# A graph network in four layers: the second layer's weight net moved into the first layer's second gather

## The chip, the cores and the metric

The program runs on one core of one Trainium2 chip (trn2). The metric is device time in microseconds, the median of the runs shown. The engines of the core are TensorE (PE, with its weight loads apart as PEld), VectorE (DVE), ScalarE (ACT), GpSimd (POOL) and SyncE (SP), and 16 DMA engines serve them.

## The reference

Four graph layers on 3125 nodes with 256 features and 100,000 edges; after each, a layer norm of x plus the layer's output. Two of them matter here.

```
# layer 0 (graph convolution)
norm = edge_weight * rsqrt(deg_out[src] * deg_in[dst] + EPS)
h6 = relu(segment_sum((x @ W6)[src] * norm, dst) + b6)
h7 = relu(segment_sum((h6 @ W7)[src] * norm, dst) + b7)
out = h7 @ Wp + bp
# layer 1, the weights of each edge
h = silu(edge_attr_8 @ fc_w1 / sqrt(8))        # 8 -> 64
h = silu(h @ fc_w2 / 8)                        # 64 -> 64
w = h @ fc_w3 / 8                              # 64 -> 256, one row per edge
```

The three lines of layer 1 are the "weight net" of this document. They depend on the edge's eight attributes and on nothing else; layer 1's later stage multiplies w with gathered rows.

## The kernel before, in words

The program is written by hand, engine by engine: each helper writes the instructions of one engine, in the order in which they run there, with semaphores between them. A meeting of all engines (`meet`) divides it into stages. Around the change they are:

1. **Preparation** (to some 2470 us). Edges are counted and ranked; POOL scatters a record of 16 numbers per edge, sorted by source (`rec_s`), then one of 8 numbers, sorted by destination (`rec_d`), to DRAM, by indirect DMAs of 128 records each (L334).
2. **The weight net** (`mlp_vector`, `mlp_sync`, `mlp_tensor`, `mlp_scalar`; L716 to L837). 832 chunks of 128 edges, in 104 groups of eight. For a group SP loads 64 KB of records (L747); PE transposes them (L771, bank 0), makes the first product in four matmuls of 128 columns (L779, bank 1), the second in one of 512 columns (L788, bank 4) and, chunk by chunk, the third, 64 rows by 256 columns (L797, banks 5 to 7). Even chunks take rows 0 to 63 of the array, odd ones rows 64 to 127. A float32 matmul stands in the profile as two passes, each with a weight load. ACT copies the transposed records (L811), applies silu (L818, L826), and writes a chunk's weights out of the bank, scaled and unscaled (L835, L837). SP stores a group, 1 MB, to `weights_dram` (L752). The steps are pipelined by numbers: in step n PE does the transposing for chunk n-5, the first product for n-7, the second for n-10 and the third for n-14. When the net is done, PE transposes the degrees (L801), DVE copies them (L728) and SP spreads them through DRAM to all partitions (L755, L757).
3. **Layer 0, first gather**: x rows are gathered (L1029), multiplied by a one-hot matrix (L1121) and added (L1086).
4. **The product with W6** (`linear_tensor`, L906 and L914; `linear_keep`, L922; `relu_bias_vector`, L935 and L937), and the store of the table h6 to DRAM (`write_table`, L890).
5. **Layer 0, second gather** (`gather_pool`, `second_vector`, `second_tensor`). POOL gathers 128 rows of h6 per chunk, 808 chunks, into a ring of 22 slots (L1160). DVE makes the weighted one-hot matrix of a chunk (L1171); PE multiplies it with the gathered rows (L1194), two chunks to a bank, eight banks; after each pair `pe.drain()` raises the semaphore `summed` (L1196). On it wait POOL, for a free slot, and DVE, which adds a chunk's sums to the block's rows (L1182), 16 chunks behind its one-hot matrices. At its start SP loads all records `rec_s` (6.6 MB) for layer 1 (L1207) and that layer's weights.
6. **Products with W7 and Wp, layer norm**, then layer 1, which waits for the records in `y_vector` (L1294), and gathers its own rows (L1363) beside the weights of each edge.

The lines of the second gather that the steps speak of:

```
pe.matmul(half_bank(c), hot20[:, c % 20, :], hg[:, c % R2, :], start=True, stop=True)
if c % 2 == 1:
    pe.drain().then_inc(summed.s, 1)
```

Of the kernel before, what the change touches and what calls it, by code (L numbers as in the profile page):

```python
# [13 lines left out]
P = 128  # L14
N, E, D = 3125, 100000, 256
NB = -(-N // P)
# [7 lines left out]
MUL = 64  # L24
# [62 lines left out]
def program(nc, t, out):  # L87
    with ExitStack() as ctx:
# [602 lines left out]
        o = 0  # L691
# [8 lines left out]
        RW = 16  # L700
        w_out = cut(acc, o, RW * D, RW, D)
        o += RW * D
# [4 lines left out]
        assert o <= DIN  # L707
        fc_all = acc[:, o - 512 - P - D:o]
        din_t, din_row = ring[0:NB, 5200:5200 + P], acc[:, DIN:DIN + NPAD]
# [10 lines left out]
        def mlp_vector():  # L720
            v.wait_ge(scattered_s.s, 16 * EJ)
            v.memset(fc_all, 0.0).then_inc(fc_zeroed.s, 1)
            v.wait_ge(fc_in.s, 16 * 18)
            then_v(v.tensor_scalar(fc3, fc3, 0.125, None, ALU.mult))
            v.tensor_scalar(fc3[:, 2 * MUL:3 * MUL], fc3[:, 2 * MUL:3 * MUL], 0.5773502691896258, None,
                            ALU.mult).then_inc(fc_scaled.s, 1)
# [3 lines left out]
        def mlp_sync():  # L730
            sp.wait_ge(scattered_s.s, 16 * EJ)
            sp.wait_ge(fc_zeroed.s, 1)
# [3 lines left out]
            for k in range(2):  # L736
                sp.dma_start(fc2[k * MUL:(k + 1) * MUL, k * MUL:(k + 1) * MUL],
                             t["L1_gnn_fc_w2"]).then_inc(fc_in.s, 16)
                for to, part in enumerate((2, 0, 3, 1)):
                    sp.dma_start(fc3[k * MUL:(k + 1) * MUL, to * MUL:(to + 1) * MUL],  # L740
                                 t["L1_gnn_fc_w3"][:, part * MUL:(part + 1) * MUL]).then_inc(fc_in.s, 16)
            for n in range(NG + 2):
# [7 lines left out]
                if i >= 0:  # L750
# [3 lines left out]
            sp.wait_ge(din_ready.s, 1)  # L754
            sp.dma_start(din_dram, din_t).then_inc(din_out.s, 16)  # L755
            sp.wait_ge(din_out.s, 16)
            sp.dma_start(din_row, din_dram.rearrange("(o b) p -> o (b p)", o=1).to_broadcast([P, NPAD])  # L757
                         ).then_inc(din_in.s, 16)

        def mlp_tensor():  # L760
            pe.wait_ge(deg_kept.s, 1)
            pe.wait_ge(fc_scaled.s, 1)
            for n in range(8 * NG + 14):
                i = n // 8
                c = n - 5
                if c >= 0 and c % 8 == 0 and c // 8 < NG:
                    i = c // 8
                    pe.wait_ge(rec_b_in.s(i, 3), rec_b_in.n(i, 3))
# [3 lines left out]
                c = n - 7  # L772
                if c >= 0 and c % 8 == 0 and c // 8 < NG:
                    i = c // 8
                    pe.wait_ge(rec_kept.s, i + 1)
                    if i >= 1:
                        pe.wait_ge(first_act.s, i)
                    for j in range(4):
                        ins = pe.matmul(ps[1][:, j * P:(j + 1) * P], fc1[:, j, :], rec_t[:, i % 2, :],  # L779
                                        start=True, stop=True)  # L780
                    ins.then_inc(first_done.s, 1)
                c = n - 10
                if c >= 0 and c % 8 == 0 and c // 8 < NG:
                    i = c // 8
                    pe.wait_ge(first_act.s, i + 1)
                    if i >= 1:
                        pe.wait_ge(second_act.s, i)
# [1393 lines left out]
```

## Time and profile before

| what | value |
|---|---|
| median of 3 runs | 10671.05 us (10670.89 to 10685.13) |
| the profiled execution, its own time | 10728.81 us |
| its span | 10726.9 us |
| mean granted clock of TensorE | 0.766 |
| PE busy | 6037.8 us, 56% |
| DVE busy | 5900.6 us, 55% |
| POOL busy | 5661.9 us, 53% |
| ACT busy | 2871.8 us, 27% |

The busy shares are means over stages with different limits; no engine is busy throughout. A row of the profile names the line, the engine, what is written and read, and the count; behind the bar stand busy time, the mean of one instruction and the engine's idle time before them with what ended it. "issue" is idle time for which the profile shows no cause. PEq is PE's sequencer, where a drain stands. A clock of 1.00 is TensorE at 2.4 GHz, 0.50 is 1.2 GHz, and a value between is a mix of the two.

### The profile page before, as it was taken

The numbers are of one execution on the slowest core, as the hardware profiler recorded it, in microseconds if no ns is written. First come the engines' busy times: TensorE is split into PE (matmuls) and PEld (weight loads), VectorE is DVE, ScalarE is ACT, GpSimd is POOL, SyncE is SP. The second block draws the span as 40 slices with busy tenths as digits, with TensorE's granted clock in tenths as the row PEclk, the third lists the DMA queues.
The fourth block names the chain that finished last, engine by engine and source line by source line (L and its number), as shares of the span: only waits on it lengthen the run. The fifth ranks groups of instructions, "written<-read, shape, count | busy, mean of one in ns | idle before, by whom it ended". The sixth has DMA issues, their size and how long they took to land. (4 is left out here: it accounts for less than half of the span.)

```text
span 10726.9 us, 101982 instructions
## 1 busy us (share of the span) xinstructions
PE 6037.8 (56%) x21277; PEld 3348.6 (31%) x21277; DVE 5900.6 (55%) x17189; ACT 2871.8 (27%) x9329; POOL 5661.9 (53%) x5879
## 2 busy tenths in 40 slices
PE   2211344446865555555556777774555578845564
PEld 1101233334433333333333111153333334333332
DVE  8925533430016666544446999946656579942223
ACT  0000000106852222100004888842222236600000
POOL 5776656561006666566652777723555520046664
PEclk9999855558986666666677999976666669966666
DMA  2000111104553333433334777734666646523333
GB/s 78 6 6 5 32 46 46 46 31 132 175 192 93 93 94 93 111 91 92 91 78 109 213 213 213 214 79 129 186 187 187 187 127 175 158 77 92 92 92 81
DMA packets 796197, 1192.44 MB, mean 111 GB/s; under 512 B 161213, under 2 KB 631923, under 8 KB 788941
## 3 DMA queue, kind: packets, MB, share of 16 engines
q0 software_dynamic: 259712, 606.96, 21.8%
q1 hardware_dynamic: 535885, 578.95, 16.7%
q8 instruction: 197, 3.23, 0.1%
q14 instruction: 403, 3.30, 0.1%
HBM read 926.73 MB, written 258.64 MB: 111 GB/s over the span
## 5 line engine op out<-in xcount | busy, mean ns | idle before, releaser
L1160 POOL DMA_INDIRECT ring<-scaled_table,idx_s x832 | 789.4, 949 | 1170.0 <-DVEq L193 771.5
L1029 POOL DMA_INDIRECT big<-x_table,rec_d_sb x808 | 808.9, 1001 | 1086.3 <-DMA x_table<-big 721.3
L1758 POOL DMA_INDIRECT ring<-att_table,rec_d_sb x808 | 776.5, 961 | 810.8 <-DVE acc L1868 277.6
L1437 PE MATMUL bank<-ring,wts 128*128 128x512 f32 x1664 | 929.6, 641 | 401.2 <-DVE acc L1424 174.3
L1363 POOL DMA_INDIRECT ring<-y_table,idx_s x832 | 805.0, 968 | 462.8 <-DVEq L193 184.0
L334 POOL DMA_INDIRECT rec_s<-acc,big x784 | 844.4, 1077 | 373.6 <-issue 253.3
L334 POOL DMA_INDIRECT rec_d<-x_res,big x784 | 753.1, 961 | 496.9 <-issue 249.1
L1160 POOL DMA_INDIRECT ring<-h_table,rec_d_sb x808 | 766.6, 949 | 454.5 <-issue 223.7
L2111 PE MATMUL bank<-ring,acc 128*128 128x256 f32 x1664 | 692.1, 558 | 522.5 <-issue 505.6
L1121 PE MATMUL bank<-big,acc 128*128 128x256 f32 x1616 | 644.5, 539 | 573.7 <-issue 450.8
L1194 PE MATMUL bank<-ring,acc 128*128 128x256 f32 x1616 | 642.1, 537 | 542.9 <-issue 477.4
L1382 ACT ACTIVATE ring<-ring,big 128x64 f32<-128x64 f32 x2496 | 686.6, 339 | 257.5 <-issue 148.6
L1777 PE MATMUL bank<-big 128*128 x2424 | 624.3, 388 | 206.6 <-issue 124.0
L1182 DVE TENSOR_TENSOR acc<-acc,bank 128x256 f32 x808 | 340.5, 421 | 615.7 <-PEq L1196 334.8
L2111 PEld LDWEIGHTS bank<-ring,acc 128*128 128x128 f32 x1664 | 407.5, 271 | 807.1 <-issue 748.7
L2101 DVE TENSOR_TENSOR acc<-acc,bank 128x256 f32 x416 | 175.2, 421 | 859.5 <-PEq L2114 656.4
L1121 PEld LDWEIGHTS bank<-big,acc 128*128 128x128 f32 x1616 | 381.6, 261 | 836.4 <-issue 787.3
L1194 PEld LDWEIGHTS bank<-ring,acc 128*128 128x128 f32 x1616 | 380.4, 261 | 804.6 <-issue 748.2
L401 ACT COPY big<-bank 128x425 f32<-128x425 f32 x49 | 25.2, 515 | 2215.2 <-PE bank L456 1659.4
L1437 PEld LDWEIGHTS bank<-ring,wts 128*128 128x128 f32 x1664 | 249.7, 189 | 1080.5 <-issue 521.1
L1996 PE MATMUL bank<-ring 128*128 128x264 f32 x1616 | 546.1, 426 | 65.5 <-issue 58.8
L1865 DVE TENSOR_TENSOR ring<-bank,wts 128x256 f32<-128x256 f32 x808 | 337.9, 418 | 441.1 <-ACT wts L1819 228.9
(346 smaller groups left out, 12793.6 us busy)
## 6 DMA issues: line engine op xcount, KB each, us to landing
weights_dram<-acc SPq DMA_DIRECT2D x104, 1024.0 KB, 4.5
ring<-weights_dram SPq DMA_DIRECT2D x832, 128.0 KB
rows_spill<-ring SPq DMA_DIRECT2D x808, 128.0 KB
big<-rows_spill SPq DMA_DIRECT2D x808, 128.0 KB, 2.2
ring<-key_dram SPq DMA_DIRECT2D x49, 1024.0 KB
big<-dl_dram SPq DMA_DIRECT2D x50, 512.0 KB
ring<-y_table,idx_s POOLq DMA_INDIRECT x832
ring<-scaled_table,idx_s POOLq DMA_INDIRECT x832
```

What stands on the lines that cost most here:

```text
L334: g.indirect_dma_start(out=table, out_offset=bass.IndirectOffsetOnAxis(ap=row_of[k][:, j:j + 1], axis=0), in_=stage[:, j, :], in_offset=No ...
L1029: g.indirect_dma_start(out=xg[:, c % RG, :], out_offset=None, in_=x_table, in_offset=bass.IndirectOffsetOnAxis(ap=recd3i[:, c, D_IDX:D_IDX ...
L1121: pe.matmul(half_bank(c), onehot[:, c % 16, :], xg[:, c % RG, 0:D], start=True, stop=True)
L1160: g.indirect_dma_start(out=slot[:, c % ring_len, :], out_offset=None, in_=table, in_offset=bass.IndirectOffsetOnAxis(ap=index(c), axis=0)) ...
L1194: pe.matmul(half_bank(c), hot20[:, c % 20, :], hg[:, c % R2, :], start=True, stop=True)
L1363: g.indirect_dma_start(out=yg[:, n % RY, :], out_offset=None, in_=y_table, in_offset=bass.IndirectOffsetOnAxis(ap=idx_s[:, n:n + 1], axis= ...
L1382: ins = a.mul(dots[:, c % 2, d * MUL:(d + 1) * MUL], vectors[:, d * MUL:(d + 1) * MUL], recs3[:, c, S_SH + 1 + d:S_SH + 2 + d])
L1437: pe.matmul(ps[6 + u % 2], oh1[c // 4 % 2][:, c % 4, :], mid[:, c % 2, 0:512], start=(c % GS == 0), stop=(c % GS == GS - 1)).then_inc(summ ...
L1758: g.indirect_dma_start(out=ag[:, n % R3, :], out_offset=None, in_=att_table, in_offset=bass.IndirectOffsetOnAxis(ap=recd3i[:, n, D_IDX:D_I ...
L1777: ins = pe.matmul(ps[c % 3][:, 0:TW], hot_n[:, i % 3, k * P:(k + 1) * P], big_b[:, bass.ds(at + s * TW, TW)], start=(s == 0), stop=(s == 2))
L1996: pe.matmul(ps[c % 8][:, 0:TW], oh3[c // 4 % OH3][:, c % 4, :], msg[:, c % 8, :], start=True, stop=True).then_inc(summed.s, 1)
L2111: pe.matmul(ps[u % 8][:, 0:D], oh20[:, c % 20, :], sg[:, c % R4, :], start=(c % 2 == 0), stop=(c % 2 == 1))
```

## The change

The net has no stage of its own any more. Its weights are loaded and scaled in the stage of the product with W6 (`mlp_weights_sync`, `mlp_weights_vector`), and its steps are woven into the second gather: before each chunk's matmul PE does one of the 846 steps, at 38 of the 808 chunks two. ACT's part runs through that stage, and SP's loads and stores too, with the load of all records behind the last store. The net has four banks left, one for transposing, first and second product together and three for the third, and the gather's sums have four instead of eight; DVE adds them eight chunks behind its one-hot matrices instead of 16. A pair's last matmul raises `summed` itself, without a drain. The degrees' transposing, copy and DMAs stand at the end of preparation. The net's output ring `w_out` lies in `big`, and the table h6 behind it.

```diff
-        def mlp_vector():
-            v.wait_ge(scattered_s.s, 16 * EJ)
-            v.memset(fc_all, 0.0).then_inc(fc_zeroed.s, 1)
+        def din_vector():
             v.wait_ge(din_turned.s, 1)
             v.tensor_copy(din_t, ps[4][0:NB, 0:P]).then_inc(din_ready.s, 1)
...
+        turned_bank, first_bank, second_bank = ps[4][:, 0:P], ps[4], ps[4]
+        third_bank = [ps[5 + c][:, 0:D] for c in range(3)]
...
-            for n in range(8 * NG + 14):
+        MLP_STEPS = 8 * NG + 14
+
+        def mlp_tensor_step(n):
...
-                    if i >= 1:
-                        pe.wait_ge(rec_kept.s, i)
-                    pe.transpose(ps[0][:, 0:P], rec_b[:, i % 3, :], ident).then_inc(rec_turned.s, 1)
+                if i >= 1:
+                    pe.wait_ge(second_act.s, i)
+                pe.transpose(turned_bank, rec_b[:, i % 3, :], ident).then_inc(rec_turned.s, 1)
...
-        mlp_vector()
-        mlp_sync()
-        mlp_tensor()
-        mlp_scalar()
-        v.wait_ge(w_stored.s(NG - 2, 2), w_stored.n(NG - 2, 2))
-        v.wait_ge(w_stored.s(NG - 1, 2), w_stored.n(NG - 1, 2))
+        din_vector()
+        din_sync()
+        din_tensor()
+        v.wait_ge(scattered_s.s, 16 * EJ)
...
         linear_scalar()
+        v.memset(fc_all, 0.0).then_inc(fc_zeroed.s, 1)
+        mlp_weights_sync()
         h6_vector()
         linear_over()
+        mlp_weights_vector()
         write_table(h6_table, h6)
...
-            for n in range(NCD + 16):
+            for n in range(NCD + 8):
...
-                c = n - 16
+                c = n - 8
...
-                    ins = v.tensor_tensor(here, here, half_bank(c), ALU.add)
+                    ins = v.tensor_tensor(here, here, quarter_bank(c), ALU.add)
...
         def second_tensor():
+            pe.wait_ge(fc_scaled.s, 1)
+            step = 0
             for c in range(NCD):
+                while step * NCD < (c + 1) * MLP_STEPS:
+                    mlp_tensor_step(step)
+                    step += 1
                 p = c // 2
                 pe.wait_ge(gathered.s(c, R2), gathered.n(c, R2))
                 if c % 2 == 0:
                     pe.wait_ge(weighed.s, weighed.n(p + 1))
-                    if p >= 8:
-                        pe.wait_ge(added.s, added.n(p - 7))
-                pe.matmul(half_bank(c), hot20[:, c % 20, :], hg[:, c % R2, :], start=True, stop=True)
+                    if p >= 4:
+                        pe.wait_ge(added.s, added.n(p - 3))
+                ins = pe.matmul(quarter_bank(c), hot20[:, c % 20, :], hg[:, c % R2, :], start=True, stop=True)
                 if c % 2 == 1:
-                    pe.drain().then_inc(summed.s, 1)
+                    ins.then_inc(summed.s, 1)
...
         def second_sync():
-            sp.wait_ge(table_out.s, table_out.n(0))
-            sp.dma_start(big[:, 0:NCS * RS], by_rank(rec_s_dram)).then_inc(rec_in.s, 16)
...
+            mlp_sync()
+            sp.wait_ge(table_out.s, table_out.n(0))
+            sp.wait_ge(w_stored.s(NG - 2, 2), w_stored.n(NG - 2, 2))
+            sp.wait_ge(w_stored.s(NG - 1, 2), w_stored.n(NG - 1, 2))
+            sp.dma_start(big[:, 0:NCS * RS], by_rank(rec_s_dram)).then_inc(rec_in.s, 16)
...
         second_tensor()
+        mlp_scalar()
```

PE's order in the net's stage before, one group of eight (each row a matmul of the program, x3 the same three times, with the semaphores that it waits for):

```order
L771 MATMUL bank<-ident,acc 128x128 [waits rec_kept,rec_b_in2]
L797 MATMUL bank<-acc 128x256 [waits w_kept]
L797 MATMUL bank<-acc 128x256 [waits w_kept,second_act]
L779 MATMUL bank<-acc 128x128 [waits first_act,rec_kept]
L779 MATMUL bank<-acc 128x128 x3
L797 MATMUL bank<-acc 128x256 [waits w_kept] x3
L788 MATMUL bank<-acc 128x512 [waits second_act,first_act]
L797 MATMUL bank<-acc 128x256 [waits w_kept] x3
```

And in the second gather now, where L1205 is the gather's matmul, L801 the net's third product, L785 the first and L792 the second:

```order
L1205 MATMUL bank<-ring,acc 128x256 [waits added,weighed,gathered10]
L785 MATMUL bank<-acc 128x128 [waits rec_kept]
L785 MATMUL bank<-acc 128x128 x3
L801 MATMUL bank<-acc 128x256 [waits w_kept]
L1205 MATMUL bank<-ring,acc 128x256 [waits gathered11]
L801 MATMUL bank<-acc 128x256 [waits w_kept]
L1205 MATMUL bank<-ring,acc 128x256 [waits added,weighed,gathered12]
L801 MATMUL bank<-acc 128x256 [waits w_kept]
L1205 MATMUL bank<-ring,acc 128x256 [waits gathered13]
L792 MATMUL bank<-acc 128x512 [waits first_act]
L801 MATMUL bank<-acc 128x256 [waits w_kept]
L1205 MATMUL bank<-ring,acc 128x256 [waits added,weighed,gathered14]
```

Third products that stood side by side now have a gather matmul between them. SP's queue from the product with W6 on, in the change: the net's weights (L740 to L746) stand ahead of the store of the table (L889), and loads and stores of groups behind the weights of layer 1.

```order
L740 DMA acc<-in_L_gnn_fc_w 8x64 [waits fc_zeroed,engines_met]
L740 DMA acc<-in_L_gnn_fc_w 8x64 x7
L743 DMA acc<-in_L_gnn_fc_w 64x64
L746 DMA acc<-in_L_gnn_fc_w 64x64 x4
L743 DMA acc<-in_L_gnn_fc_w 64x64
L746 DMA acc<-in_L_gnn_fc_w 64x64 x4
L889 DMA h_table<-big 128x25x256 [waits table_ready]
```

Before, nothing stood between the meeting and that store on this queue, and the load of all records came right behind it.

## Rows read from the trace of the kernel before

**Rows 1.** Stretches: length; busy PE, PEld, DVE, ACT, POOL; clock; DMA share; GB/s.
```profile
2471.00:3144.00 673.00, 557.62 (x2793) 326.97 (x2791) 0.28 (x1) 533.91 (x1972) 0.34 (x1) 0.97 0.52 173
4431.00:5606.00 1175.00, 642.09 (x1616) 380.39 (x1616) 559.31 (x1601) 0.00 (x0) 766.65 (x808) 0.68 0.34 97
5800.00:7000.00 1200.00, 867.74 (x1558) 232.30 (x1556) 1103.19 (x3308) 974.72 (x3306) 852.63 (x973) 1.00 0.73 213
```
**Rows 2.** Timeline of POOL (start, duration, in us), the last scatter.
```profile
2470.38 0.96 POOL L334 DMA_INDIRECT rec_d<-x_res,big  x1 [0.30 <-issue]
```
**Rows 3.** Timeline of DVE, the first instruction after the net's stage.
```profile
3144.52 5.39 DVE L1035 MEMSET x_res<- 128x6400 f32 x1 [6.07 <-issue]
```
**Rows 4.** Waits, second gather, 4431 to 5612 us (total, times, longest).
```profile
PE bank L1194 <- issue: 477.4, 366, 7.4
```
**Rows 5.** Timeline of POOL inside the second gather.
```profile
5001.79 0.95 POOL L1160 DMA_INDIRECT ring<-h_table,rec_d_sb  x1 [0.30 <-issue]
...
5006.08 0.95 POOL L1160 DMA_INDIRECT ring<-h_table,rec_d_sb  x1 [2.10 <-PEq L1196]
```
**Rows 6.** Timeline of PE at the same place (x4 is one pair).
```profile
5006.02 2.04 PE L1194 MATMUL bank<-ring,acc 128*128 128x256 f32 x4 [6.00 <-issue]
5008.29 2.04 PE L1194 MATMUL bank<-ring,acc 128*128 128x256 f32 x4 [0.23 <-issue]
```
**Rows 7.** By line: shortest/median/longest in ns, first and last start in us.
```profile
L1160 POOL DMA_INDIRECT ring<-h_table,rec_d_sb x808: 943/949/1009, 4431.8 to 5586.8; - x162
...
L1182 DVE TENSOR_TENSOR acc<-acc,bank x808: 420/422/423, 4451.0 to 5605.9; 128x256 f32 x162
...
L1196 PEldq DRAIN  x404: 952/2047/8945, 4448.4 to 5603.2; - x135
```
**Rows 8.** DMA issues: KB each, median us to landing.
```profile
weights_dram<-acc SPq DMA_DIRECT2D x104, 1024.0 KB, 4.5
...
big<-rows_spill SPq DMA_DIRECT2D x808, 128.0 KB, 2.2
```
**Rows 9.** Timeline of SP: four of the net's weight loads; the table's store.
```profile
2454.84 4.97 SPq L740 DMA_DIRECT2D acc<-in_L_gnn_fc_w  x4
...
4420.16 0.36 SPq L890 DMA_DIRECT2D h_table<-big  x1
```
**Rows 10.** The gather's start: stretch as in rows 1; PE's second chunk.
```profile
4431.00:4459.00 28.00, 9.73 (x19) 5.54 (x20) 5.60 (x17) 0.00 (x0) 20.83 (x22) 0.50 0.93 348
...
4448.45 1.22 PE L1194 MATMUL bank<-ring,acc 128*128 128x256 f32 x2 [5.03 <-DMA ring<-h_table,rec_d_sb]
```
**Rows 11.** Timeline of PE in the product with W6, at full clock.
```profile
4395.93 1.03 PE L914 MATMUL bank<-wts,ring 128*128 128x256 f32 x4
4396.80 0.38 PE L906 MATMUL bank<-ident,acc 128*128 128x128 f32 x2
```
**Rows 12.** Timeline of PE in the net's stage, one group.
```profile
2800.61 0.33 PE L771 MATMUL bank<-ident,acc 128*128 128x128 f32 x1 [1.06 <-DMA acc<-rec_s]
2800.86 0.70 PE L797 MATMUL bank<-acc 64*128 64x256 f32 x4
2801.50 1.16 PE L779 MATMUL bank<-acc 128*128 128x128 f32 x8
2802.58 1.13 PE L797 MATMUL bank<-acc 64*128 64x256 f32 x6
2803.64 1.13 PE L788 MATMUL bank<-acc 128*128 128x512 f32 x2
2804.70 1.13 PE L797 MATMUL bank<-acc 64*128 64x256 f32 x6
```
**Rows 13.** PE's unexplained waits in layer 1's gather and layer 2's sums.
```profile
PE bank L1437 <- issue: 74.9, 90, 1.6
...
PE bank L1996 <- issue: 58.8, 60, 1.5
```
**Rows 14.** Timeline of DVE, the first use of the loaded records.
```profile
5684.03 0.88 DVE L1295 COPY idx_s<-big 128x832 int32<-128x832 int32 x1 [0.19 <-POOLq L193]
```

More of the change, by code:

```diff
@@ L753, in mlp_sync @@
                                  w_out[:, 8 * (i % 2):8 * (i % 2) + 8, :]).then_inc(w_stored.s(i, 2), 16)
[L754 to L762, printed above, removed]
-            for n in range(8 * NG + 14):
[L764 to L768, printed above, removed]
-                    if i >= 1:
-                        pe.wait_ge(rec_kept.s, i)
-                    pe.transpose(ps[0][:, 0:P], rec_b[:, i % 3, :], ident).then_inc(rec_turned.s, 1)
[L772 to L787, printed above, removed]
-                    pe.matmul(ps[4], fc2, h1[:, i % 2, :], start=True, stop=True).then_inc(second_done.s, 1)
-                c = n - 14
-                if 0 <= c < NCS:
-                    i, k = c // 8, c % 8
-                    half = slice((k % 2) * MUL, (k % 2) * MUL + MUL)
-                    if k == 0:
-                        pe.wait_ge(second_act.s, i + 1)
-                    if c >= 3:
-                        pe.wait_ge(w_kept.s, c - 2)
-                    pe.matmul(ps[5 + c % 3][:, 0:D], h2[half, i % 2, (k // 2) * P:(k // 2) * P + P],
-                              fc3[half, :], start=True, stop=True).then_inc(third_done.s, 1)
-            pe.wait_ge(deg_kept.s, 1)
-            pe.wait_ge(second_act.s, NG)
-            pe.transpose(ps[4][0:NB, 0:P], deg_d[:, 0:NB], ident).then_inc(din_turned.s, 1)
@@ new lines, in program @@
+        MLP_STEPS = 8 * NG + 14
+        def mlp_tensor_step(n):
+            c = n - 5
+            if c >= 0 and c % 8 == 0 and c // 8 < NG:
+                i = c // 8
+                pe.wait_ge(rec_b_in.s(i, 3), rec_b_in.n(i, 3))
+                if i >= 1:
+                    pe.wait_ge(second_act.s, i)
+                pe.transpose(turned_bank, rec_b[:, i % 3, :], ident).then_inc(rec_turned.s, 1)
+            c = n - 7
+            if c >= 0 and c % 8 == 0 and c // 8 < NG:
+                i = c // 8
+                pe.wait_ge(rec_kept.s, i + 1)
+                for j in range(4):
+                    ins = pe.matmul(first_bank[:, j * P:(j + 1) * P], fc1[:, j, :], rec_t[:, i % 2, :],
+                                    start=True, stop=True)
+                ins.then_inc(first_done.s, 1)
+            c = n - 10
+            if c >= 0 and c % 8 == 0 and c // 8 < NG:
+                i = c // 8
+                pe.wait_ge(first_act.s, i + 1)
+                pe.matmul(second_bank, fc2, h1[:, i % 2, :], start=True, stop=True).then_inc(second_done.s, 1)
+            c = n - 14
+            if 0 <= c < NCS:
+                i, k = c // 8, c % 8
+                half = slice((k % 2) * MUL, (k % 2) * MUL + MUL)
+                if k == 0:
+                    pe.wait_ge(second_act.s, i + 1)
+                if c >= 3:
+                    pe.wait_ge(w_kept.s, c - 2)
+                pe.matmul(third_bank[c % 3], h2[half, i % 2, (k // 2) * P:(k // 2) * P + P],
+                          fc3[half, :], start=True, stop=True).then_inc(third_done.s, 1)
@@ L803, in mlp_scalar @@
         def mlp_scalar():
-            for n in range(8 * NG + 14):
+            for n in range(MLP_STEPS):
                 c = n - 5
@@ L810, in mlp_scalar @@
                         a.wait_ge(first_done.s, i - 1)
-                    a.copy(rec_t[:, i % 2, :], ps[0][:, 0:P]).then_inc(rec_kept.s, 1)
+                    a.copy(rec_t[:, i % 2, :], turned_bank).then_inc(rec_kept.s, 1)
                 c = n - 7
```

42 lines of the change are left out of this document (27 added, 15 removed).

## The prediction

> **What bounds the kernel now.** I read the table of stretches first, since one core runs a row of stages divided by meetings of all engines, and a stage is worth what its own last wait is worth [rows 1]. Three stretches matter. The weight net of the second layer (2471 to 3144 us) is a stage in which POOL is idle (one instruction), DVE is idle, and PE and ACT work alone at a granted clock of 0.97. The second gather of the first layer (4431 to 5606) has the opposite mix: ACT idle, POOL 767 us, PE 642 us at a clock of 0.68, DVE 559 us. The third is the second layer's own gather (5800 to 7000), a witness: it moves 213 GB/s with a DMA share of 0.73, and POOL still issues 778 gathers in 1200 us.
>
> Then I read where the net's stage begins and ends. POOL's last scatter of destination records starts at 2470.38 [rows 2]; and DVE opens the next stage with a memset at 3144.52, after 6.07 us of idling in which the last stores land [rows 3]. Only the last few scatters overlap the net.
>
> Last, the gather: PE's unexplained waits of 477.4 us in 366 places [rows 4], then a piece of the timeline. POOL needs 0.95 us for a gather and 0.30 to the next while nothing holds it, and then waits 2.10 us for PE's sequencer, which frees ring slots [rows 5]. At that moment PE has started nothing for 6.00 us [rows 6]: the wait ends for both when a drain ends. The 404 drains reach 8.9 us, with a median of 2.05 [rows 7]. So POOL could do the 808 gathers in 808 x 1.2525 = 1012 us; from first to last they take 1155 (4431.8 to 5586.8) [rows 7], because PE stops now and then at a drain.
>
> **The change, part by part.** The sum is made on the profiled execution, 10728.8 us, which is 57.8 above the median of the three runs.
>
> *The net's stage goes: 670 us saved.* DVE now enters the meeting when the last destination scatter has landed. Its issue starts at 2470.38; a landing takes between 2.2 us (rows read back from the spill) and 4.5 us (a store of 1 MB) [rows 8]. I take the small end, since a scatter moves 4 KB, and 1 us for the meeting: the memset starts near 2474 instead of 3144.5, so 670, with 668 and 671 as ends. The transposing of the degrees, DVE's copy and the two DMAs go ahead of it, on PE, DVE and SP, which wait there for nothing but the scatters. The broadcast of 1.6 MB thereby leaves the window in which x and the records are loaded. It is worth between 0 and 5 us (1.6 MB at the 348 GB/s of [rows 10]); I take 3.
>
> *The weights of the net are loaded under the first product: 1 us lost.* DVE's memset of 896 columns stands ahead of its first addition, which waits for PE's first product anyway. The 18 DMAs stand on SP ahead of the store of the table: four took 4.97 us to issue, so 18 take 22 [rows 9]. They start near 4390 and end near 4412; SP's next work, the table's store, was issued at 4420.16 [rows 9]. Cover is 8 us; were SP twice as slow, the table would be 14 us late. DVE's two short scalings come after its last block and only delay its entry to the meeting, while the table is still on its way. Ends 0 and 14; I take 1.
>
> *The gather takes the net's work.* Its terms, engine by engine.
> POOL: unchanged, 1012 us if never held.
> PE, at full clock: a pass of 256 columns takes 0.217 us (four from 4395.93 to 4396.80, and between full-height products of different kinds nothing is lost) [rows 11]. A chunk of the gather is two passes, 0.434, x 808 = 351 us. A third-layer product of the net is two such passes too. In the old stage it costs less: three of them take 1.06 us (2802.58 to 2803.64) [rows 12], since two neighbours use different halves of the rows and run at once: 0.43 for the two, 0.43 for the third, and 0.2 left, which I read as two changes between half-height and full-height at 0.1 each. In the new order a gather chunk, of full height, stands between any two of them, except at some 38 places where two steps fall together (846 steps on 808 chunks). So 832 x 0.434 = 361 us, plus two changes per chunk, 808 x 0.2 = 162. Per group of eight, the first product takes 1.08, the second 1.06 and the transpose 0.25 [rows 12]; less one change each, counted already, 2.09 x 104 = 217. Less 38 x 0.5 for the neighbours that still pair: PE needs 351 + 361 + 162 + 217 - 19 = 1072 us.
> The Trainium skill (TensorE: Matmul & The Clock Gate, "Part 3: Packing small matmuls") says that matmuls in different row groups run at once in the array. By it this interleaving gives away a gain which the old stage had, and the trace agrees: three products in 1.06 us, where two gather chunks take 0.87.
> ACT: 534 us in the old stage [rows 1]; it has 1080 now, and what waits for it stands three or four steps, 4 to 5 us, behind its cause. Hidden.
> DVE: 559 us for 808 chunks [rows 1], 1.4 per pair. PE may now be only three pairs ahead of it instead of seven; that is still 8 us. Hidden; if DVE fell behind, PE and with it POOL would wait for the banks.
> SP and the DMAs: a store of 1 MB, landing in 4.5 us [rows 8], and a load of 64 KB per eight steps, now every 10.4 us instead of 6.5. In the old stage PE waited 1.06 us for such a load [rows 12], with a group every 6.5 us (673/104); with one every 10.4 the same eight steps of lead leave 3 us to spare. SP's own waits for `w_kept` hold nothing else on its queue but loads and stores of the net and, last, the records' load. The share of DMA becomes 0.34 x 1175/1080 + 0.52 x 673/1080 = 0.69, under the witness's 0.73.
> The drain goes: a matmul tells of its own end, as in the witness and in the sums of the third layer, and there PE's unexplained waits are never longer than 1.6 and 1.5 us [rows 13], against 7.4 here [rows 4]. I count no stall of that kind. The clock: PE has work for 1072 of 1080 us, which is more than in the net's stage with 0.97 and the witness with 1.00 [rows 1], so full clock.
> The largest is PE with 1072. The load of 6.6 MB of records no longer stands beside the first gathers (the second chunk was used only at 4448.45) [rows 10]; PE begins near 4434.5, a landing after POOL, and DVE ends 2 us behind PE. End: 4434.5 + 1072 + 2 = 5508 instead of 5606.3: 98 saved. Ends: 156 saved when POOL bounds (1012 + 7 us), 288 lost when the old stalls return whole (second rival).
>
> *The records' load* is issued when the last store has landed, some 6 us after the gather. The one beside the first gathers was over within the 28 us of [rows 10], and DVE uses it 78 us after the gather's end, at 5684.03 [rows 14]. Hidden; without that cover, 34 us.
>
> Sum: 10728.8 - 670 - 3 + 1 - 98 = 9959, less 57.8: **9901 us**.
>
> **Rivals.**
> *POOL is the bound.* If the changes of height cost nothing, PE needs 910 us and POOL sets the end at 1012 + 7: 9901 - 58 = 9843. For it: the pure pace of [rows 11]. Against: the 0.2 us in [rows 12].
> *The stalls belong to the gather, not to the drain.* Then 477 - 404 x 0.23 (the ordinary drain [rows 6]) = 384 us are added to a PE that is now the bound: 9901 + 384 = 10285; half of them give 10093. For: all three stages with stalls gather through POOL. Against: so does the witness, without any.
> *Stores and gathers add.* While 6.6 MB were loaded beside the first gathers, the DMA share was 0.93 and PE waited 5.03 us for the second chunk [rows 10]. Were every store to hold the gathers for its 4.5 us, POOL's 1012 would grow by 468, to 1480: 10300. The ring of 22 chunks (27 us) speaks against it. The Trainium skill (DMA: Bandwidth & Descriptors, "Queues, rings and completion order") has each DMA engine take whole packets from one queue before it turns to the next; by that rule a store gets more than half of an engine, which is this case in a milder form, and the start of the gather agrees with it.
> *The clock stays at its low level: slower.* If PE runs the woven stream at 1.2 GHz, as it does for much of the gather now (clock 0.68), passes double: 2 x (351 + 361 + 217 - 19) + 162 = 1982 us, a stage of 1989, 814 longer than now: 10671 - 672 + 814 = 10813. It decides from a stage of 1847 us on, that is with the low level over more than 85% of it. For: short waits on ACT, SP and POOL are spread through the stream. Against: the net's stage has the same waits and 0.97.
> *The stage is not freed.* Something under the net other than its own work would have to end late; [rows 2] show nothing.
>
> **How the numbers follow.** PE-bound as computed, 0.55 (9870 to 9960); POOL-bound, 0.20; stalls return in part or whole, 0.14; stores and gathers add, 0.05; low clock, 0.04; not freed, 0.02. A measurement of this kernel tells 0.2%, 21 us, from no change. Faster 0.95, same 0.01, slower 0.04. The range runs from 9830 (POOL-bound, with the small terms at their good ends) to 10080, which takes in stalls up to nearly half and leaves out some 0.18.
>
> **What would show it.** DVE's memset of x near 2474; no net rows before 3000 us. In the gather: duration near 1078, clock above 0.95, POOL's waits on PE's matmuls some 60 us in all, PE's idle small with no wait over 3 us, the third product's passes 0.22 apart and 0.3 before a gather chunk. Wrong: a gather over 1250 us, a clock under 0.85, PE waits of 4 us and more, or POOL never waiting.

## Result, and the profile after

The changed kernel takes 10135.2 us (median of four runs, 10106.9 to 10168.3) against 10671.6 for the one before: a ratio of 0.949, 95% interval 0.947 to 0.952. 536 us are saved where 770 were foretold. The profiled execution took 10106.9 us, its span is 10105.0. The net's old stage is gone as foretold; the second gather, which was to become 98 us shorter, became 110 longer.

The two traces side by side, by first and last starts on their timelines (us, from the span's start):

| stretch | before | after | change | foretold |
|---|---|---|---|---|
| start to POOL's last scatter | 2470.4 | 2459.5 | -10.9 | 0 |
| from there to the first gather of x | 722.2 | 55.4 | -666.8 | -673 |
| first gather stage, to the product with W6 | 1197.0 | 1195.2 | -1.8 | 0 |
| product, table, to the second gather's first | 42.2 | 42.8 | +0.6 | +1 |
| second gather, to DVE's last addition | 1174.5 | 1284.2 | +109.7 | -98 |
| layer 2, to the products after its gather | 1486.1 | 1492.0 | +5.9 | 0 |
| those products, to the next stage's first gather | 246.4 | 185.4 | -61.0 | 0 |
| the rest | 3388.1 | 3390.5 | +2.4 | 0 |

The row of -61 is no work of the change. Its products, 600 passes after layer 2's gather, are the same in both kernels; the table of stretches (columns as in [rows 1]) shows their clock, before and after:

```profile
7088.00:7230.00 142.00, 135.01 (x600) 125.05 (x600) 23.76 (x56) 44.89 (x152) 0.00 (x0) 0.51 0.00 1
```
```profile
6524.00:6604.00 80.00, 73.98 (x600) 70.28 (x600) 23.52 (x54) 43.78 (x147) 0.00 (x0) 0.98 0.00 1
```

600 passes at clock 0.51 take 135 us, at 0.98 they take 74. The level differs from one execution to the next, with no tie to the change: in the trace of `before_again` (below), the same kernel as before, the passes take 75 us at clock 0.97, and the row from them to the next gather is 185 us, as after the change. So the execution profiled before had most likely a slow draw of this stage; it lay 57 us above its median; the one after lies 28 below its own, for a reason that its trace alone does not show. So 621.9 (span to span) - 57 - 28 = 537, the 536 of the medians.

The stretches of the second gather after the change:

```profile
3753.00:3853.00 100.00, 68.26 (x150) 35.18 (x150) 22.07 (x64) 17.50 (x53) 51.08 (x54) 0.57 0.32 95
3853.00:4996.00 1143.00, 1138.68 (x4159) 601.38 (x4159) 522.21 (x1504) 542.64 (x1870) 712.12 (x753) 1.00 0.60 182
4996.00:5037.00 41.00, 38.02 (x117) 19.62 (x117) 13.84 (x39) 15.62 (x55) 2.12 (x3) 0.88 0.47 102
```

For 1143 us (the middle row) PE is busy nearly all the time (1138.68) at full clock, as foretold, and yet gets only 753 chunks done: 1.518 us each, not the 1072/808 = 1.327 of the prediction. The first 100 us carry 32 chunks (51 us lost against the steady pace), the last 41 carry 23 (6 lost). 808 x 1.518 + 51 + 6 = 1284.

The stage by line (busy, mean in ns | idle before, releasers), and PE's waits (total, times, longest) in it:

```profile
L1162 POOL DMA_INDIRECT ring<-h_table,rec_d_sb x808 | 765.4, 947 | 550.0 <-PE bank L1205 275.8 <-issue 202.7 <-DMA h_table<-big 66.8
L1205 PE MATMUL bank<-ring,acc 128*128 128x256 f32 x1616 | 576.7, 440 | 18.5 <-DMA ring<-h_table,rec_d_sb 16.9 <-issue 1.6
L801 PE MATMUL bank<-acc 64*128 64x256 f32 x1664 | 575.4, 436 | 0.0
```
```profile
PE bank L1205 <- DMA ring<-h_table,rec_d_sb: 16.9, 2, 16.5
PE bank L779 <- issue: 14.5, 1, 14.5
PE bank L785 <- ACT acc L812: 8.6, 1, 8.6
PE bank L792 <- ACT acc L819: 5.1, 4, 2.7
```

The 477 us of unexplained waits of [rows 4] have shrunk to some 17, all but one of them short; POOL now waits 276 us for PE's sums, where some 60 were foretold. The stage is bound by PE. PE's timeline shows where its time goes (start, duration):

```profile
4205.93 0.70 PE L801 MATMUL bank<-acc 64*128 64x256 f32 x2
4206.56 0.70 PE L1205 MATMUL bank<-ring,acc 128*128 128x256 f32 x2
4207.09 1.05 PE L785 MATMUL bank<-acc 128*128 128x128 f32 x8
4208.08 0.70 PE L801 MATMUL bank<-acc 64*128 64x256 f32 x2
4208.70 0.70 PE L1205 MATMUL bank<-ring,acc 128*128 128x256 f32 x2
4209.33 0.70 PE L801 MATMUL bank<-acc 64*128 64x256 f32 x2
```

From a half-height product (64 rows, L801) to a full-height one (L1205) and back it is 0.63 us each time. Two passes of 256 columns are 0.434 [rows 11], so a change of height costs some 0.19, not the 0.1 of the prediction.

### The profile page after: what moved, and what is told of

The parts are those of the page before. It is cut to its first block and busy times, and to the rows that moved or that the text cites. A ratio compares the mean times of both kernels' runs of the same rounds, so it can differ in the third digit from the quotient of the medians.

```text
span 10105.0 us, 101372 instructions
## 1 busy us (share of the span) xinstructions
PE 6039.2 (60%) x21277; PEld 3249.0 (32%) x21277; DVE 5884.0 (58%) x17189; ACT 2904.1 (29%) x9330; POOL 5654.3 (56%) x5879
## 5 line engine op out<-in xcount | busy, mean ns | idle before, releaser
L2126 PE MATMUL bank<-ring,acc 128*128 128x256 f32 x1664 | 695.6, 560 | 519.8 <-issue 500.6
L2126 PEld LDWEIGHTS bank<-ring,acc 128*128 128x128 f32 x1664 | 409.0, 272 | 806.4 <-issue 744.9
L1834 ACT ACTIVATE wts<-bank 128x256 f32<-128x256 f32 x808 | 302.7, 383 | 1001.7 <-remote 460.3
L1205 PE MATMUL bank<-ring,acc 128*128 128x256 f32 x1616 | 576.7, 440 | 18.5 <-DMA ring<-h_table,rec_d_sb 16.9
```

Source lines behind the costliest of these rows:

```text
L1205: ins = pe.matmul(quarter_bank(c), hot20[:, c % 20, :], hg[:, c % R2, :], start=True, stop=True)
L2126: pe.matmul(ps[u % 8][:, 0:D], oh20[:, c % 20, :], sg[:, c % R4, :], start=(c % 2 == 0), stop=(c % 2 == 1))
```

## Experiments

The result and the experiments fall into six sets of runs. In each set the kernel before was timed on the same chip as the others, and its times are of two kinds: 10671, 10624, 10629 and 10675 us in four sets (the first is that of the result above), 8989 and 8991 in two. The five sets of the experiments ran on five different chips, none of them twice, so whether those are two sorts of chip or one in two conditions, the runs cannot tell. I call them the *late* and the *prompt* condition, for a reason that the traces give below. Ratios are against the kernel before of the same set. A length given for the gather runs from POOL's first gather to DVE's last addition. Where no ratio is given below, a kernel ran only once (full_nogather, before_nogather, before_again, filler_again, nogather_again, filler_2, nogather_2).

### Full height, pairs, and the drain

**full_height**: zeros fill the other half of the weights, so every product has 128 rows.

```diff
-        fc2, fc3 = acc[:, o:o + P], acc[:, o + P:o + P + D]
+        fc2, fc3 = acc[:, o:o + P], acc[:, o + P:o + P + 2 * D]
...
-                pe.matmul(third_bank[c % 3], h2[half, i % 2, (k // 2) * P:(k // 2) * P + P],
-                          fc3[half, :], start=True, stop=True).then_inc(third_done.s, 1)
+                pe.matmul(third_bank[c % 3], h2[:, i % 2, (k // 2) * P:(k // 2) * P + P],
+                          fc3[:, (k % 2) * D:(k % 2) * D + D], start=True, stop=True).then_inc(third_done.s, 1)
```

> The changed kernel, but each third-layer product runs over all 128 rows against weights whose other half is zero, so that PE never changes between half-height and full-height products; their number, order, waits and banks stay. Theory H (each change of height costs 0.19 us on PE, two per chunk): PE needs 0.87 + 2.1/8 = 1.13 us per chunk, POOL with its 1.2525 sets the pace, the second gather shrinks from 1284 us to 1012 plus some 45 for its start, about 1060, and the kernel takes 9880 to 9940. Rival S (the 0.19 us belongs to any switch between two kinds of product, with its bank and its semaphore wait): nothing changes, 1284 us and 10107 to 10168.

Measured (late condition): 10019.3 us, ratio 0.9436 (0.9414 to 0.9458); gather 1226 us. PE and ACT on the timeline:

```profile
4209.88 0.59 PE L801 MATMUL bank<-acc 128*128 128x256 f32 x2
4210.31 0.59 PE L1205 MATMUL bank<-ring,acc 128*128 128x256 f32 x2
...
4210.74 1.05 PE L786 MATMUL bank<-acc 128*128 128x128 f32 x8
...
4211.63 0.60 PE L801 MATMUL bank<-acc 128*128 128x256 f32 x2
4212.06 0.59 PE L1205 MATMUL bank<-ring,acc 128*128 128x256 f32 x2
...
4213.79 0.59 PE L1205 MATMUL bank<-ring,acc 128*128 128x256 f32 x2
4215.65 0.60 ACT L819 ACTIVATE acc<-bank 128x512 f32<-128x512 f32 x1 [4.62 <-issue]
4216.30 1.13 PE L793 MATMUL bank<-acc 128*128 128x512 f32 x2 [1.91 <-issue]
```

Products of the same kinds, in the same order, with the same waits, now start 0.43 us apart. So the 0.19 belongs to the change of height alone: theory H is right on the cost, and S falls. But the stage did not shrink to 1060. Something new shows: the first-layer product (L786) was issued by 4211.6, and ACT's L819, which waits for its end and had nothing else to do, starts at 4215.65. PE then waits for ACT in turn. In 32 of the 104 groups L819 starts over 3 us after the last of these passes, with ACT idle. (The steady part of the changed kernel has 13 such places in the trace of the result and none in `after_again`; PE had other work there and stood still for 1 us at most.)

The rows of the weight loads (PEld) differ too, first in the changed kernel, then in full_height:

```profile
4206.55 0.30 PEld L1205 LDWEIGHTS bank<-ring,acc 128*128 128x128 f32 x2 [0.33 <-issue]
```
```profile
4210.09 0.41 PEld L1205 LDWEIGHTS bank<-ring,acc 128*128 128x128 f32 x2
```

After a half-height product the load starts with its own matmul (4206.56), after a full-height one 0.22 us ahead of it (4210.31). The Trainium skill (TensorE: Matmul & The Clock Gate, "Part 3: Packing small matmuls") says that weights are pulled ahead of running matmuls if the row groups don't conflict or the load goes to the background buffer. Two full-height products use the same rows, and there the load was pulled ahead, as the second condition allows; at a change of height it was not, and which of the page's two conditions fails there no run here shows.

**pairs**: the net's steps are taken two at a time, ahead of every even chunk.

```diff
-                while step * NCD < (c + 1) * MLP_STEPS:
+                while c % 2 == 0 and step * NCD < (c + 2) * MLP_STEPS:
```

> The changed kernel, but the net's steps are taken two at a time ahead of every even chunk, so that two neighbouring third-layer products (on different halves of the rows) stand together, and then two chunks. Theory H with products on different rows running at once, as in the net's old stage: per pair of chunks PE needs 0.87 + 0.43 + 2 x 0.19 + 0.52 = 2.2 us, 1.1 per chunk, POOL sets the pace, gather about 1060 us, kernel 9880 to 9940. If the two do not run at once here: 2.64 per pair, 1.32 per chunk, gather about 1110, kernel 9940 to 10000. If the chain through ACT and the three banks holds PE: gather 1200 and more.

Measured (late): 10075.5 us, ratio 0.948 (0.9456 to 0.9505); gather 1274 us. The third outcome came true. Some neighbours do run at once (the first row: four passes in the time of two), others are parted, and PE stands before them:

```profile
4304.82 0.70 PE L801 MATMUL bank<-acc 64*128 64x256 f32 x4
4305.45 1.13 PE L1205 MATMUL bank<-ring,acc 128*128 128x256 f32 x4
...
4309.44 0.70 PE L801 MATMUL bank<-acc 64*128 64x256 f32 x2
...
4310.75 0.69 PE L801 MATMUL bank<-acc 64*128 64x256 f32 x2 [0.61 <-issue]
```

With three banks a product must wait for ACT to empty the bank that the third one before it filled; here ACT's answer came too late.

**drain_back**: the changed kernel with the drain behind every second gather product.

```diff
-                    ins.then_inc(summed.s, 1)
+                    pe.drain().then_inc(summed.s, 1)
```

> The changed kernel with the drain after every second gather product put back. If the drain is what stalled PE before (theory D): its ordinary 0.2 us x 404 = 90 us and stalls up to 384 us come on top of 1284: gather 1400 to 1760, kernel 10230 to 10600. If the stalls belonged to a gather whose PE runs now at the low and now at the high clock (theory G), only the ordinary cost returns, as PE is now at full clock all the way: gather about 1375, kernel 10200 to 10260.

Measured (late): 10150.6 us, ratio 0.9549 (0.9531 to 0.9567); gather 1367 us against 1281 for the changed kernel in the set of `after_again`. That is 86 us, 0.21 per drain: only the ordinary cost. Theory G's length of the gather (1375) is met, D's is not; the time of the whole lies below both forecasts. What G says of a changing clock is not shown by this: the late answer in full_height above came while PE's passes stood 0.22 us apart, at full clock.

**before_nodrain**: the kernel before, where only this drain is gone (the same edit in reverse).

> The kernel before, where only the drain of the second gather is replaced by an increment on the second product itself; eight banks and the net's own stage stay. Theory D: the waits of 477 us go, POOL sets the pace, the gather shrinks from 1175 to about 1040 us and the kernel takes about 10535. Theory G: stalls of 4 to 7 us stay, gather 1100 to 1175, kernel 10600 to 10671.

Measured (late): 10573.2 us, ratio 0.9949 (0.9932 to 0.9966); gather 1159 us against 1164 for the kernel before in `before_again`. D's 1040 did not come; the whole, too, lies below G's 10600, and nearer to D's 10535. But the stage hardly moved, so the 51 us that the whole saved are not the stage's; where they are from stays open (the products of the -61 above vary by as much between runs). The stalls stay without any drain:

```profile
4752.16 1.10 PE L1194 MATMUL bank<-ring,acc 128*128 128x256 f32 x4 [1.47 <-DVE acc L1182]
...
4757.22 0.94 POOL L1160 DMA_INDIRECT ring<-h_table,rec_d_sb  x1 [0.30 <-issue]
4760.80 0.94 POOL L1160 DMA_INDIRECT ring<-h_table,rec_d_sb  x1 [2.64 <-remote]
4761.86 0.42 DVE L1182 TENSOR_TENSOR acc<-acc,bank 128x256 f32 x1 [9.60 <-issue]
...
4763.30 1.19 PE L1194 MATMUL bank<-ring,acc 128*128 128x256 f32 x2 [10.04 <-DVE acc L1182]
```

PE's products were issued by 4752.9. DVE, which waits here for the semaphore `summed` alone, makes its next addition at 4761.86, 9.6 us after its last work; the trace's record of that semaphore, which lacks some increments in the late condition (373 of 404 stand here), has the one that frees DVE at 4760.54. The drain only made such a delay visible as its own duration; theory D falls. The Trainium skill (Perfetto Trace Analysis, "Per-engine timelines") says that a matmul's end is an estimate of the profile, and that its increment goes out when PSUM has acknowledged the write. The traces agree that an increment can come long after the end shown; at which of the steps it is held, no run here shows.

### A second condition

> The full-height kernel (label full_height) without the 808 gathers of the second gather: POOL does nothing there, the products take a ring of ones that DVE sets once. With the gathers, PE's increments reached ACT and DVE up to 4 to 8 us after its products about every 11 us, though the products had been issued. Theory P (PE holds its completions back by itself, after a few us of products back to back): the same late increments and gaps of 2 to 4 us before the second-layer product stay, stage 1100 to 1200 us. Rival Q (the gathers, their DMAs or POOL's work hold PE up): they go, and PE runs through at 1.13 us per chunk, about 930 us with a slow start.

> The kernel before without the 808 gathers of its second gather (a ring of ones in their place); drains and eight banks stay. Theory P: the waits of 4 to 7 us at drains stay; at DVE's pace of 0.87 us per chunk the stage would be 700 us, with the stalls 1000 or more, and the clock goes up and down as before. Rival Q: no wait over 2 us, some 720 us.

The two kernels leave out the gathers (their sums are sums of ones). Their edit:

```diff
+            then_v(v.memset(hg, 1.0))
...
-                pe.wait_ge(gathered.s(c, R2), gathered.n(c, R2))
...
-        gather_pool(hg, h6_table, lambda c: recd3i[:, c, D_IDX:D_IDX + 1], NCD, R2)
```

> The kernel before with four banks and no drain in the second gather, and one more product per chunk, whose sum nobody reads: PE has 0.87 us of work per chunk at full clock, steadily, under POOL's 1.2525. If the stalls come with the changes of the clock and a steady load avoids them (theory C): clock over 0.95, no wait of 4 us, POOL sets the pace, gather about 1030 us, kernel 130 us faster than before. If load itself brings the stalls (theory P): they stay or grow, gather 1150 to 1350 us.

The product that it adds, beside the four banks and the missing drain:

```diff
+                pe.matmul(ps[4 + c % 4][:, 0:D], hot20[:, c % 20, :], hg[:, c % R2, :], start=True, stop=True)
```

**best**, the full-height kernel with the drains of the first and the last gather replaced as well:

> The full-height kernel, and the drains of the other two gathers (the first one and the last) also replaced by increments on the product itself. Theory D (a drain costs by itself): 0.2 us x 820 lie on PE, which waits in both stages; up to 100 us less. Theory N (they are hidden, and the late increments stay, as in the kernel before without its drain): 0 to 20 us less than full_height, kernel 0.94 of before.

These four met the prompt condition: the kernel before took 8989.0 us. full_nogather took 8881.4 (stage 906 us, PE at 1.12 us per chunk, as worked out), before_nogather 8726.5 (stage 758), before_filler 8990.5, ratio 1.0009 (0.9986 to 1.0033), gather 1021; best 8984.8, ratio 0.999 (0.9967 to 1.0013), gather 1024. There were no late increments to explain (in before_filler and best each of the 404 increments of `summed` is on record within 0.6 us of the start of the pass that raises it), so the theories P, Q and C stayed open. But three other things came out. First, in `best` POOL sets the pace, 1024 us for the 1012 + 7 of the rival "POOL is the bound":

```profile
3346.00:4370.00 1024.00, 943.05 (x4424) 760.67 (x4424) 566.15 (x1607) 562.55 (x1977) 764.09 (x808) 0.98 0.71 217
```

Second, its increments in place of the drains elsewhere gave nothing here: its last gather takes 1056 us with or without drains (before_filler has them). Third, where the net stands in before_filler, which has it in its old place:

```profile
1339.00:2041.00 702.00, 589.10 (x2809) 347.74 (x2808) 0.28 (x1) 533.82 (x1977) 520.37 (x544) 0.94 0.54 167
```

POOL is busy 520 us of it. In the prompt condition PE and DVE are done with their part of the sorting at 1315 us, and not at 2420; POOL's scatters go on to 2170, and the net runs wholly beside them. The stage that the change removes is then free of charge: from the last scatter to the first gather of x it is 55.5 us there (2169.9 to 2225.5), and 56.2 in the changed kernel of `after_third` below (2166.4 to 2222.6).

### The change in the prompt condition

> The kernel before, for a trace on the same chip as the next two. The last four runs came from a chip on which the kernel before takes 8989 us, not 10671: PE's increments are prompt there, and by the trace of before_filler the net's stage ran from 1339 to 2040 us, wholly beside POOL's scatters, which end at 2171. If this chip is like that one: about 8990 us, net over by 2045, second gather about 1030 us. If it is like the first: 10600 to 10730, net from about 2460, second gather 1160 to 1175.

> The changed kernel. On a chip like the first: 0.949 of before, gather about 1280 us. On a chip with prompt increments the net costs nothing in its old place, and the change only brings PE's 1.50 us per chunk into the gather: 808 x 1.504 + 20 = 1235 us in place of 1030, so some 200 us SLOWER than before, about 9190 us (1.022).

> The full-height kernel of the first call, on this chip beside the changed kernel. On a chip with prompt increments: gather 1030 us, POOL's pace, 8990 us, 200 less than the changed kernel and level with before. On a chip like the first: 90 to 120 us less than the changed kernel, gather about 1215, since late increments stop PE 2 to 4 us at a time.

The set met the late condition (before 10629.3). before_again: 10608.8 us, gather 1164. after_again: 10068.2, ratio 0.9473 (0.943 to 0.9515), gather 1281. full_again: 10025.3, ratio 0.9423 (0.9379 to 0.9467), gather 1238. So the full-height kernel saves 43 us on the change (runs 10000 to 10042 against 10056 to 10073), half of what I had written.

> The changed kernel once more, to meet the other kind of chip (the one on which the kernel before takes 8989 us). There, as written for after_again: net's old place free of charge, gather 1235 in place of 1030 us, about 9190 us, 1.02 of before. On a chip like the first: 0.947 to 0.949 of before.

This set met the prompt one (before 8991.1): after_third took 9191.5 us, ratio 1.0224 (1.0207 to 1.0242). The same change is **slower** there, by 200 us where 200 were expected. Its gather:

```profile
3345.00:4579.00 1234.00, 1221.76 (x4425) 649.14 (x4426) 558.81 (x1607) 584.22 (x1977) 763.06 (x808) 0.99 0.59 180
```

1234 us against 1021 in before_filler. 100 of its 1234 us carry 66 chunks (DVE makes 727 in the 1100 us from 3400), 1.513 each, so 808 take 1223, and only 11 us are lost at its ends in place of 57.

### Is PE held by the gathers, and does slack help?

**slack** adds to the full-height kernel:

```diff
-        turned_bank, first_bank, second_bank = ps[4][:, 0:P], ps[4], ps[4]
-        third_bank = [ps[5 + c][:, 0:D] for c in range(3)]
+        turned_bank, first_bank, second_bank = ps[4][:, 0:P], ps[4], ps[7]
+        third_bank = [ps[(3, 5, 6)[c // 2]][:, c % 2 * D:c % 2 * D + D] for c in range(6)]
...
-            c = n - 10
+            c = n - 13
...
-            c = n - 14
+            c = n - 19
```

> The full-height kernel with more room between PE and ACT: third-layer products go by pairs into three banks (six in flight in place of three), gather sums have three banks, the second-layer product a bank of its own, and stands six steps behind the first (not three), the third six behind the second, with four slots for the records and stores one group later. Theory L (late increments only hurt where PE waits for an answer): PE runs on through them, POOL sets the pace, gather 1040 to 1100 us, kernel 0.925 to 0.93 of before on a chip like the first. Theory R (PE itself stands still in those 4 us): PE has 1.13 us of work per 1.48 us as now, gather 1180 to 1230, kernel 0.942. On the other kind of chip 1030 us and 8990 either way.

> The same file as before_filler, whose run fell on the chip with prompt increments and so said nothing of the stalls. On a chip like the first: theory C (steady load avoids them) clock over 0.95 and a gather of 1030 to 1060 us; theory P (load brings them) 1150 to 1350.

> The same file as before_nogather, for the same reason. On a chip like the first: theory P (PE's increments are late by PE's own doing) the stage takes 900 us or more with waits of 4 us and longer at drains; rival Q (the gathers hold PE up) 720 to 760 us and no wait over 2.

Prompt condition: slack 8984.3 us, ratio 0.9982 (0.9964 to 1.0), gather 1024; filler_again 8986.2, gather 1022; nogather_again 8719.7, stage 758. The same three files once more:

> The same file as slack, in another call, since the last one fell on the chip with prompt increments. On a chip like the first: theory L (late increments only hurt where PE waits for an answer) gather 1040 to 1100 us, 0.925 to 0.93 of before; theory R (PE itself stands still) 1180 to 1230, 0.942.

> On a chip like the first: theory C (a steady load of PE avoids the stalls) clock over 0.95 and a gather of 1030 to 1060 us; theory P (load brings them) 1150 to 1350.

> On a chip like the first: theory P (PE's increments are late by PE's own doing) 900 us or more, with waits of 4 us and longer at drains; rival Q (the gathers hold PE up) 720 to 760 us and no wait over 2.

This time the condition was late (before 10675.2). slack_2: 10054.6 us, ratio 0.9426 (0.941 to 0.9442), gather 1225. The slack gives nothing, as theory R has it in numbers. That PE stands still by itself is not shown: most of its idle time in slack_2 ends with an answer that it had to wait for, that of ACT (L821, the first silu) before the transposing, which shares a bank with the first product, and those of DVE, whose sums have one bank less here. PE's waits (total, times, longest):

```profile
PE bank L780 <- ACT acc L821: 96.4, 58, 3.3
PE bank L1207 <- DVE acc L1175: 32.4, 18, 2.6
PE bank L1207 <- DVE acc L1186: 29.1, 32, 3.9
```

(3870 to 4990 us; PE's other waits there come to some 25.) So the room was widened at some steps and narrowed at DVE's sums, and theory L had no fair trial. filler_2: 10679.3 us, gather 1188, clock 0.84, waits up to 7 us: a heavier and steadier load does not avoid the stalls, so C falls here, and P's number is met. nogather_2 speaks against P all the same. Its stage, and that of nogather_again in the prompt condition:

```profile
4432.00:5191.00 759.00, 501.53 (x1618) 303.78 (x1619) 548.77 (x1615) 0.00 (x0) 0.00 (x0) 0.91 0.02 9
```
```profile
3348.00:4107.00 759.00, 502.44 (x1616) 304.04 (x1616) 549.16 (x1616) 0.00 (x0) 0.00 (x0) 0.90 0.02 9
```

Without gathers the two conditions differ by nothing, drains and all; no two of PE's passes are over 2.5 us apart. With them the same kernel's stage differs by 167 us (filler_2 1188, filler_again 1022). So in this stage the late increments come with POOL's gathers: rival Q. That holds for the kernel before; full_nogather, with nearly twice as much work on PE, did not meet the late condition. Nor are gathers enough: layer 2 gathers through POOL too, and its gather takes about as long in both conditions (figures at the end). By what road a gather holds back PE's increments stays open. In 57 of the 66 gaps of PE over 3 us in filler_2 no gather had moved a packet for 1 us or more when PE went on, and POOL had waited for a free slot, but in before_again only in 37 of 84; an empty queue may as well follow from the stall. That PE waits at similar places in the sorting, beside POOL's scatters, fits, and no run tried it.

## Why the prediction was right and where it was wrong

*The net's stage goes, 670.* Right in the late condition, if 6 us too good: DVE's memset of x stands at 2470.61, 11 us after the last scatter's issue and not 4, and 666.8 us are gone from there to the first gather of x, where 673 were foretold. [rows 2] could not show that this cost depends on when PE and DVE finish the sorting; in the prompt condition it is nil. I gave "the stage is not freed" 0.02, on the ground that nothing else ends late under the net. That is the wrong question: the stage cost time only because PE came to it late, and why PE came late (it waited, unexplained, in the sorting too) I did not ask.

*Weights under the product, records' load.* +0.6 where +1 was foretold; the records' load is hidden, since from the gather's end to layer 2 nothing changed.

*The gather, -98: the step that failed.* Term by term: the passes (351 and 361), POOL's 1012, ACT, DVE and SP are as worked out; ACT and DVE do not hold PE in the steady part. The term "two changes per chunk, 808 x 0.2 = 162" was mis-sized. It is 808 x 2 x 0.19 = 307, and explains 145 of the 155 between 1072 and 808 x 1.518 = 1227. The rows had it: in [rows 12] a third product after a pair takes 0.43 + 0.43 + 0.20, and I took the 0.20 for two changes. It is one, at the end of that window; the other lies ahead of 2802.58, in the 1.08 us of the eight short passes. The pair at 2800.86 with 0.64 until L779, holding only one change, would have settled it: 0.64 - 0.43 = 0.21.

*The start of the gather.* I let the gather start without loss. In the late condition 51 us were lost in the first 100: PE met two waits of 14.5 and 8.6 us there, and ran 78 us at the low level of its clock (0.50), until 3853. What held up ACT in those waits the trace does not say. In the prompt condition both ends together lost 11.

*No stall counted, clock full.* Both came true, 1.00 over 1143 us. But the reason was wrong: not the drain, for drain_back has no stalls of PE with it in its steady part, and before_nodrain has them without it. PE of the changed kernel is free of them in its steady part, where it is always behind the gathers, and has them at its start; the late answers themselves are not all gone (the 13 places above). Why being behind should help was not tested.

*The rivals.* "POOL is the bound" (0.20) needed changes of height that cost nothing; made true in `best` and `slack`, in the prompt condition, it gave 1024 us. "The stalls belong to the gather, not to the drain" (0.14) names the right cause with a wrong consequence: 384 us were not added. "Stores and gathers add" would need POOL slowed; it waited for PE, and in `best`, beside the same stores, it kept its own pace. The slower rival, the low clock, did not come; the slower outcome that exists has another mechanism, the free stage.

Together: 208 us of the gather's error (145 + 10 for PE's steady pace, 51 + 6 at its ends, less 4 counted for the ends). The medians add 28, since the profiled execution of the changed kernel lies that far below its median. The other rows of the first table come to 60 us less than foretold, the -61 nearly alone, and cancel against the 58 that the sum had taken off for the profiled execution before: 10135 instead of 9901, outside the range of 9830 to 10080.

## What to carry to other kernels

Before you price a stage at its length, ask what its first instruction waited for; a stage that begins late because an engine was held up elsewhere may be worth nothing when that engine is not. When half-height and full-height products are woven together, every change costs PE 0.19 us, two for each small product that stands alone; filling the small ones up with zeros to full height added no passes and took all of it away. Read a transition's cost from two windows that hold one and two transitions: from a single window you cannot tell how many halves of it you have caught.

The version to keep is the full-height one: 0.942 to 0.944 of before in the late condition, where the change alone gives 0.947 to 0.949, and, as `best` and `slack`, level with before in the prompt one (0.998 to 0.999), where the change alone gives 1.022. full_height itself did not meet the prompt condition.

## What was new of the hardware

- The same kernel before takes 8989 or 10671 us by the condition that the runs meet. The difference lies in stages where POOL issues scatters or gathers: the second gather 1021 against 1164 us (before_filler, before_again; its own trace in the prompt condition was not taken), the last one 1056 against 1195, while layer 2's gather, with 1318 and 1323, hardly differs. PE's part of the sorting ends at 1315 us (before_filler), and in the late condition at 2421 (before) or 2373 (before_again).
- PE's increments can reach waiting engines 4 to 10 us after its products have been issued. The drain does not bring this about by itself: with all its drains the stage takes 758.4 us without gathers in both conditions. Whether a heavier load of PE does, without gathers, was not met in the late condition.
- A change between products of 64 and of 128 rows costs 0.19 us at full clock; a drain behind every second gather product costs 0.21 (86 us for 404) where PE is the bound.
